# Turning the hidden rows of shared experts by four DMAs and a VectorE block transpose instead of on TensorE

## What is computed

```python
def _swiglu(t, wa, wb, wo):
    h = jax.nn.silu(t @ wa.T) * (t @ wb.T)
    return h @ wo.T
weights, indices = jax.lax.top_k(scores, TOP_K)
for e in range(N_EXPERTS):
    w_e = jnp.sum(jnp.where(indices == e, weights, 0.0), axis=-1)
    y = y + _swiglu(t, w1[e], w3[e], w2[e]) * w_e[:, None]
z = _swiglu(t, sw1, sw3, sw2)
return (y + z).reshape(shape)
```

## Time and profile before

| | |
|---|---|
| median of 3 runs | 741.99 us (741.28 to 747.87) |
| span of the profiled execution | 739.8 us |
| TensorE busy (matmul) | 717.1 us, 97% |
| VectorE busy | 568.5 us, 77% |
| ScalarE busy | 459.4 us, 62% |
| GpSimd busy | 363.4 us, 49% |
| the second part | 210 to 740 us |
| HBM | 253 GB/s over the span |

### The profile page before, as it was taken

How to read it: one execution, slowest core, us unless ns; L and a number is a source line. 1 busy time by engine, 2 the same in 40 slices (tenths; PEclk the granted TensorE clock), 3 DMA queues, 4 the chain that set the end, 5 groups by cost and what they waited for, 6 DMA issues and landing times.

```text
span 739.8 us, 15553 instructions
## 1 busy us (share of the span) xinstructions
PE 717.1 (97%) x4602; PEld 676.3 (91%) x4602; DVE 568.5 (77%) x1111; ACT 459.4 (62%) x659; POOL 363.4 (49%) x190
## 2 busy tenths in 40 slices
PE   3999999999999999999999999999999999999998
PEld 3999999999998999899989999988989999999997
DVE  7899999999965578428899588848987699679942
ACT  6575757575432222126878588847885789578931
POOL 4999888887401065042435433543634354434320
PEclk9999999999999999999999999999999999999999
DMA  6678687877522122463667577766565764432101
GB/s 231 215 239 288 218 272 216 279 218 253 186 85 60 29 43 29 144 197 90 161 201 218 131 232 210 198 176 168 145 182 160 176 193 90 74 68 46 30 1 57
DMA packets 48404, 114.88 MB, mean 155 GB/s; under 512 B 7472, under 2 KB 8624, under 8 KB 48336
## 3 DMA queue, kind: packets, MB, share of 16 engines
q1 hardware_dynamic: 35792, 89.67, 37.1%
q0 software_dynamic: 12544, 24.40, 17.9%
HBM read 157.78 MB, written 29.26 MB: 253 GB/s over the span
## 4 chain that ended last, share of the span: by engine, by line
PE 69%; DVE 13%; DMA 6%; issue 5%; ACT 3%; SPq 1%; ACTq 1%; POOL 1%; DVEq 1%; POOLq 0%
PE pair L1303 19%; PE bank L1303 15%; PE pair L1328 12%; PE pair L1234 8%; PE bank L1328 6%; PE bank L1185 4%; PE pair L1311 3%; DMA out<-ys,slot_info 3%; DMA raw<-in_weights 2%; PE bank L1245 2%; DVE prod L829 2%; DVE bank L834 2%; DVE x L800 2%; DVE w_lo L1150 1%; DVE rows L841 1%
## 5 line engine op out<-in xcount | busy, mean ns | idle before, releaser
L1150 DVE TENSOR_TENSOR w_lo<-raw,w_hi 128x1408 fp32r<-128x1408 f32 x94 | 148.5, 1621 | 47.0 <-ACT w_hi L733 47.0
L1441 POOL DMA_INDIRECT out<-ys,slot_info x47 | 80.6, 1714 | 120.6 <-ACT ys L721 87.3
L1428 POOL DMA_INDIRECT tn<-t_rows,slot_info x47 | 75.5, 1605 | 123.1 <-DVE tT_lo L888 90.6
L733 ACT ACTIVATE w_hi<-raw 128x1408 fp32r x94 | 124.6, 1374 | 2.1 <-issue 1.4
L1234 PE MATMUL pair<-kv_hi,toep_hi 128*128 128x288 f32 x320 | 100.6, 314 | 1.7 <-DMA toep_lo<-kpad_lo 1.4
L1234 PE MATMUL pair<-kv_lo,toep_hi 128*128 128x288 f32 x320 | 95.3, 298 | 0.0
L1234 PE MATMUL pair<-kv_hi,toep_lo 128*128 128x288 f32 x320 | 95.1, 297 | 0.0
L1155 DVE TENSOR_TENSOR w_lo<-raw,w_hi 128x1536 fp32r<-128x1536 f32 x47 | 82.3, 1752 | 4.5 <-ACT w_hi L740 4.5
L1379 POOL TENSOR_TENSOR kv_lo<-kv,kv_hi 128x2304 fp32r<-128x2304 f32 x15 | 77.3, 5153 | 5.9 <-ACT kv_hi L625 5.9
L740 ACT ACTIVATE w_hi<-raw 128x1536 fp32r x47 | 69.3, 1474 | 0.1
L829 DVE TENSOR_TENSOR prod<-pair,q 128x256 f32<-128x256 f32 x128 | 53.4, 417 | 15.1 <-PE pair L1234 9.6
(11 more groups left out here) (223 smaller groups left out, 2009.3 us busy)
## 6 DMA issues: line engine op xcount, KB each, us to landing
raw<-in_weights SPq DMA_DIRECT2D x94, 704.0 KB
raw<-in_weights SPq DMA_DIRECT2D x47, 768.0 KB
toep_hi<-kpad_hi SPq DMA_DIRECT2D x15, 512.0 KB, 4.6
toep_lo<-kpad_lo SPq DMA_DIRECT2D x15, 512.0 KB, 6.2
cx<-in_ctx SPq DMA_DIRECT2D x15, 384.0 KB, 6.3
stage<-in_weights SPq DMA_DIRECT2D x16, 272.0 KB, 6.7
xt<-in_x SPq DMA_DIRECT2D x16, 256.0 KB, 6.4
xr<-in_x SPq DMA_DIRECT2D x16, 256.0 KB, 6.6
```

The source lines that it names most:

```text
L733: act.activation(w_hi[s % 2][:, a:b], raw[:, bass.ds(half + a, b - a)], ACT.Copy).then_inc(hi_ok[n_], 1)
L1150: dve.tensor_tensor(w_lo[s % 2][:, a:b], raw[:, bass.ds(half + a, b - a)], w_hi[s % 2][:, a:b].bitcast(F32), ALU.subtract).then_inc(lo_ok[ ...
L1428: pool.indirect_dma_start(out=tn[o % 3][:], out_offset=None, in_=t_rows, in_offset=bass.IndirectOffsetOnAxis(ap=slot_info[:, 3 * i:3 * i + ...
L1441: pool.indirect_dma_start(out=out, out_offset=bass.IndirectOffsetOnAxis(ap=rows, axis=0), in_=ys[o % 2][:], in_offset=None, bounds_check=R ...
```

## The change

For shared units alone the turn leaves TensorE. After VectorE's product, ScalarE issues four DMAs, one for each quarter of 88 columns of `hid`. DMA g moves 128 rows of 88 numbers into partitions 32g to 32g+31 of a new tile `spread`, four tokens to a partition, each with 96 columns (88 and 8 zeros). VectorE then turns blocks of 32x32 of `spread` (one instruction over 384 columns) back into `hid`. ScalarE and VectorE make `hT_hi` and `hT_lo` from `hid` in SBUF instead of from `ps_ht` in PSUM. The rows of the shared second weight are put into the order that this gives, outside the kernel's time. Routed units keep the turn on TensorE, under a new semaphore `row_turned`. Silu of unit n waits for `hT_lo` of unit n-2 instead of its turn.

```diff
+            def spread_hidden(m):
+
+                act.wait_ge(hid_ok, m + 1)
+                wait(act, hid_turned, shared_to(m) - 1)
+                for g in range(4):
+                    act.dma_start(spread[32 * g:32 * g + 32, :].rearrange("p (t c) -> p t c", t=4)[:, :, 0:QUAD],
+                                  hid[m % 2][:, g * QUAD:(g + 1) * QUAD]).then_inc(hid_spread, 16)
...
+                if unit(n - 1) and not UNITS[n - 1].routed:
+                    spread_hidden(n - 1)
                 if (s := split_down_at(n)) is not None:
...
                 if unit(n):
-                    wait(act, hid_turned, n - 1)
-                    if n < 2:
-                        act.wait_ge(hid_zero, 2)
+                    wait(act, hTl_ok, n - 1)
                     act.wait_ge(up_ok, n + 1)
...
-                    act.wait_ge(hid_turned, m + 1)
-                    act.activation(hT_hi[m % 2][:], ps_ht[:, 0:IPAD], ACT.Copy).then_inc(hTh_ok, 1)
+                    if UNITS[m].routed:
+                        act.wait_ge(row_turned, routed_to(m))
+                        src = ps_ht[:, 0:IPAD]
+                    else:
+                        act.wait_ge(hid_turned, shared_to(m))
+                        src = hid[m % 2][:]
+                    act.activation(hT_hi[m % 2][:], src, ACT.Copy).then_inc(hTh_ok, 1)
...
-            dve.memset(hid[0][:, INTER:IPAD], 0.0).then_inc(hid_zero, 1)
-            dve.memset(hid[1][:, INTER:IPAD], 0.0).then_inc(hid_zero, 1)
-            dve.wait_ge(hid_zero, 2)
+            dve.memset(view(spread[:], QUAD, [[QPAD, 4], [1, QPAD - QUAD]]), 0.0).then_inc(hid_zero, 1)
+            dve.wait_ge(hid_zero, 1)
...
+                    src = ps_ht[:, 0:IPAD] if UNITS[m].routed else hid[m % 2][:]
+                    if not UNITS[m].routed:
+                        dve.wait_ge(hid_spread, 64 * shared_to(m))
+                        dve.transpose(view(hid[m % 2][:], 0, [[1, 4], [P, ICH], [4, 32]]),
+                                      view(spread[:], 0, [[QPAD, 4], [32, ICH], [1, 32]])).then_inc(hid_turned, 1)
                     dve.wait_ge(hTh_ok, m + 1)
-                    dve.tensor_tensor(hT_lo[m % 2][:], ps_ht[:, 0:IPAD], hT_hi[m % 2][:].bitcast(F32),
+                    dve.tensor_tensor(hT_lo[m % 2][:], src, hT_hi[m % 2][:].bitcast(F32),
                                       ALU.subtract).then_inc(hTl_ok, 1)
...
-                if unit(n - 1):
+                if unit(n - 1) and UNITS[n - 1].routed:
                     turn_hidden(n - 1)
```

More of the change, by code:

```diff
@@ L46 @@
 IPAD = ICH * P
+QUAD, QPAD = INTER // 4, IPAD // 4
 W2 = ICH * L
@@ L229, in program @@
         hid = sb2("hid", [P, IPAD])
+        spread = sb("spread", [P, IPAD])
         hT_hi = sb2("hT_hi", [P, IPAD], F32R)
@@ L295, in program @@
         up_ok, silu_ok, hid_ok = sem("up_ok"), sem("silu_ok"), sem("hid_ok")
-        hid_turned, hTh_ok, hTl_ok, down_ok = sem("hid_turned"), sem("hTh_ok"), sem("hTl_ok"), sem("down_ok")
+        hid_spread, hid_turned, row_turned, hTh_ok, hTl_ok, down_ok = sem("hid_spread"), sem("hid_turned"), sem("row_turned"), sem("hTh_ok"), sem("hTl_ok"), sem("down_ok")
         y_ok = sem("y_ok")
@@ L358, in last_unit, with shared_to, routed_to @@
             return max((u.n for u in UNITS if u.o == o), default=-1)
+        def shared_to(n):
+            return sum(not u.routed for u in UNITS[:n + 1])
+        def routed_to(n):
+            return n + 1 - shared_to(n)
         def half_of(eng, s):
@@ L1311, in turn_hidden @@
                     last = pe.transpose(ps_ht[:, c * P:(c + 1) * P], hid[n % 2][:, c * P:(c + 1) * P], ident[:])
-                last.then_inc(hid_turned, 1)
+                last.then_inc(row_turned, 1)
             def down(u):
@@ L1482, in down, with down_spread @@
         return w.reshape(-1, ICH, P, L).transpose(0, 2, 1, 3).reshape(-1, P, W2)
+    def down_spread(w2):
+        w = np.zeros((w2.shape[0], 4, QPAD, L), w2.dtype)
+        w[:, :, :QUAD] = w2.transpose(0, 2, 1).reshape(-1, 4, QUAD, L)
+        return w.reshape(-1, 4, ICH, 32, L).transpose(0, 1, 3, 2, 4).reshape(-1, P, W2)
     sw1, sw3 = (a("L0_ffn_" + n).reshape(SHARED, INTER, L) for n in ("sw1", "sw3"))
@@ L1486 @@
     routed = np.concatenate([up(a("L0_ffn_w1"), a("L0_ffn_w3")), down(a("L0_ffn_w2"))], 2)
-    shared = np.concatenate([up(sw1, sw3), down(sw2)], 2)
+    shared = np.concatenate([up(sw1, sw3), down_spread(sw2)], 2)
     shared = shared.transpose(1, 0, 2).reshape(P, TILES, STAGE).transpose(1, 0, 2).reshape(SHARED * P, WROW)
```

## The result

The changed kernel takes 770.88 us in the median of 4 runs (768.97 to 773.63), the kernel before 741.63 in the same series: ratio 1.0384, 95% interval 1.0334 to 1.0434. It is 3.8% slower, where 0.9% was forecast, and above the forecast's range. The profiled execution spans 769.1 us instead of 739.8, so its trace holds 29.3 us of loss.

A forecast was written before the change was run, and what follows sets the result against it. TensorE, working almost the whole span, was taken as the bound; -1.2 - 1.7 + 2.0 - 1.6 - 1.0 - 2.6 = -6.1 took the span from 739.8 to 745.9, the median to 748.1, written 748.5; 8-in-10 range 738.5 to 760.

The forecast's parts named there:

- lead, with the clock, to unit 12: Lead stage: VectorE's backlog makes down of unit 9 late, losing 1.2 us, and the lower clock after TensorE's stop 1.7.
- units 12 to 17: Late lead stage: six turns taken off TensorE, from units 11 to 16, gain 2.0 us.
- entry to the routed stage, 18 to 24: Start of routed work: blocked hT_hi delays ScalarE's next splits, up of unit 22 waits; 1.6 us lost.
- the pairs, 24 to 75: Four pairs of shared units in the routed stage: 0.5 gained at one, 0.5 lost at each other; -1.0 us.
- end: Last units: two turns gain 0.65, late down of unit 78 loses 2.3, lower clock 1.0; net -2.6 us.
- The set's landing: Each shared unit's four DMAs: landed 3.2 us after the first begins, 4.0 among weight loads (bounds 3.2 and 6.3).
- Its own sign of being wrong: Routed stage: the forecast is wrong if landings among weight loads exceed 5 us.
- rival 3: Entries into routed work: landing among weight loads takes 6.3 instead of 4.0 us, some 12 us lost, 760; chance 0.18.
- Starts earlier by at most the eight turns before (2.6): VectorE's stretch without a gap, 270.5 to 284 us: it starts up to 2.6 us earlier, from eight turns removed.
- The transpose: VectorE's block transpose of 384 columns: taken as 0.55 us, bounded by 0.54 and 1.2.
- The ceiling: Whole kernel: 32 turns of shared units at 0.32 to 0.33 us each can gain at most 10.4 us, 1.4%.
- rival 1: Whole kernel: all added work is hidden except at the end, giving 734.5 us, 1% faster; chance 0.10.

The follow-up runs named there:

- few: Kernel before with only units 11 to 16, 75 and 76 turned by the DMAs and block transpose; ratio 1.005.
- lead_from3: Kernel before with only shared units 3 to 19 turned by the DMAs and block transpose, units 0 to 2 by TensorE; ratio 1.014.
- lo_from_sbuf: Kernel before, with hT_lo of shared units subtracting from hid in SBUF instead of PSUM, TensorE still turning; ratio 1.006.
- pairs_noadd: Only the eight paired shared units among routed ones turned by DMA, GpSimd's adding DMAs and their waits removed; 0.989 to the kernel before.
- before_noadd: Kernel before without GpSimd's adding DMAs of the rows and the waits for them; ratio 0.989.
- turn_out: Changed kernel without the four DMAs and the block transpose, hT made from unturned hid in SBUF; 0.996 to the kernel before.
- one_dma: Changed kernel with one DMA of the four per shared unit; 1.014 to the kernel before.
- lead_only: Kernel before with only units 0 to 19 turned by the DMAs and block transpose, later ones by TensorE; ratio 1.027.
- issues_only: Kernel before with four ScalarE DMAs per shared unit added into a tile nobody reads; ratio 1.002.

## Why the prediction was wrong

The mechanism held: an in-order ScalarE and VectorE that wait for the set, a stop of TensorE with a lower clock, slow two-operand instructions, and a longer tail. The sizes and one coupling did not. Step by step (us of the span; minus is a loss):

| step of the sum | predicted | measured in the changed kernel |
|---|---|---|
| lead, with the clock, to unit 12 | -2.9 | -11.1 |
| units 12 to 17 | +2.0 | +1.7 |
| entry to the routed stage, 18 to 24 | -1.6 | -3.3 |
| the pairs, 24 to 75 | -1.0 | -13.9 |
| end | -2.6 | -2.9 |

**The set's landing** is the term of which most came. It was priced at 3.2 us from the first issue (4.0 in the routed stage), by a 64 KB load that landed in 1.8 us and issues 0.46 us apart. Measured: a DMA alone lands in 2.0 us, so that price was about right, but the issues take 0.62, and a set took 3.9 to 5.8 us in the lead stage, 4.8 to 6.3 in the pairs, and 9.0 (few 11.5) behind the first weight loads. The prediction said that a step of 6.2 us hides the landing easily; with the transpose and `hT_hi` behind it only a set near 4 us is hidden. Its own sign of being wrong, landings over 5 us among weight loads, came. The bound of 6.3 us and rival 3, which gave 760, were the right side; "ScalarE's queue holds nothing else" was the reason for not taking it, and few refutes that: a queue of its own doesn't keep a set from landing late.

**"Starts earlier by at most the eight turns before (2.6)"** failed. VectorE's product in step 9 began 2.7 us later (272.37 against 269.63), since the routing work of step 1 waited for the first set; lead_from3 shows it. I had read VectorE's gaps in steps 8 to 10 and not those of step 1. From there to the end of `hT_lo` of unit 9 VectorE took 18.8 us instead of 11.8. The 7.0 more are two transposes with their waits for `hT_hi` (1.52 + 1.49, predicted 2.1), 2.45 for the slow `hT_lo` (predicted 2.2), 0.7 for `tT_lo` and 0.9 until the set came (both not predicted). The clock's share at this place was right: `down` of unit 9 lost 3.78 - 2.08 = 1.7. That it fell at four more places (some 7 us in all by the estimate above) was not in the sum.

**The transpose** was taken as 0.55, the cheaper end, and measured 0.86. The Trainium skill's figure ("VectorE: DVE Perf Modes", The three transpose paths) gave, from bf16, the estimate of 0.93, and the trace agrees with it better than with my row. The Trainium skill's rule ("SBUF — State Buffer", Who interferes with whom) on two SBUF inputs beside GpSimd is borne out by lo_from_sbuf, 2.90 against 0.55 us.

**The pairs** were priced as if each stood alone, by the slack at the last one. That price was about right where no adding DMA holds ScalarE: pairs_noadd loses nothing against before_noadd. What was left out is ScalarE's wait for a free `ys`, 30.4 us in the routed stage of the kernel before. As I read it, the lead that a pair uses up is what covered those waits, and they come back as waits for `w_lo` units later. How much each single stall owes to the set and how much to an adding DMA that happened to take long can't be told from these runs.

**The ceiling**, 10.4 us, counted 32 turns on a TensorE that is 97% busy. The turns were worth some 7 (turn_out against lo_from_sbuf), but with the operand in SBUF that the change needs, turn_out gains 1.8 in its trace (0.4% by the ratio). Even free DMAs and a free transpose would not have made rival 1 come true, which needed 1%.

**The end** came out near its sum partly by luck. No lower clock showed: after a stop of 2.6 us the granted clock read 1.00 from 763 to 766 us, where 1.0 us of loss was taken. The set was complete 4.0 us after its first issue (3.2 taken) and the transpose took 0.86 (0.55 taken), which makes up for most of it.

## What to carry to other kernels

Before a handover between engines gets a DMA in it, compare the set's whole time, all issues plus the landing of the last, with the shortest step that is to hide it; once it is longer, in-order engines pass the rest on. Look for the slack in every step in which the waiting engine has other work behind it, not only in the busiest, and for waits on that engine that use the same slack. What is taken off an engine that is 97% busy pays only if what replaces it is free elsewhere: here one operand moved from PSUM to SBUF cost 5.2 of the 7.0 us that the turns were worth.

## What the runs showed of the hardware

- A DMA of 44 KB within SBUF landed 2.0 us after its issue (median, one_dma), one of 48 KB in sets of four 2.1 (lead_only). The last of a set landed 2.05 to 3.9 us after its issue in the lead stage and 2.9 to 4.2 in the pairs (changed kernel). Beside 2.2 MB of weight loads issued just before in another queue it was 7.1 (changed kernel), 9.2 (lead_from3) and 9.55 (few).
- Four issues hold ScalarE 2.5 us, and this alone cost nothing that could be measured (issues_only, 1.002).
- A VectorE block transpose of 128x384 fp32 takes 0.86 us, of 128x32 0.21; with the short one the kernel was still 2.8% slower.
- `hT_lo` of 128x384 took 0.55 us with one operand in PSUM and up to 3.00 with both in SBUF while GpSimd multiplied; `tT_lo` behind it went from 2.56 to 3.25.
- After a stop of TensorE of 6.8 us the granted clock read 0.66 for the next 5 us, a mixture of the 2.4 and 1.2 GHz levels; after the stop of 2.6 us at the end it read 1.00.
